# Band attention with a feed-forward network on one Trainium2 core: queries and keys as fp16 halves, and a reordered first batch

## The reference

```python
xn = layernorm(x)
Q, K, V = xn @ Wq + bq, xn @ Wk + bk, xn @ Wv + bv      # 16 heads of 64 columns
scores = einsum('bhid,bhjd->bhij', Q, K)
columns = where(|i - j| <= 64, scores, 0.0)             # outside the band the score is 0, not -inf
out = softmax(columns) @ V                              # so every row still sums over all 1024 columns
attn = out @ Wo + bo
s = xn @ Win + bin_                                     # 512 -> 64
h = relu(s[..., None] * W1 + b1)                        # 16 hidden units for each of the 64
ffn = (einsum('btmh,mh->btm', h, W2) + b2) @ Wout + bout
result = x + attn + ffn
```

## Time and profile before

| | |
|---|---|
| median of three runs | 1953.55 us |
| the profiled execution's own time | 1958.2 us |
| its span, first to last instruction | 1956.5 us |
| busy: PE, PEld, DVE, ACT, POOL | 96%, 52%, 80%, 77%, 82% |
| mean granted TensorE clock | 0.983 |
| score matmuls (L1228), 128 x 12 pairs of heads, mean of one | 283 to 314 ns |
| weight loads of the projections (L1242), fp16, 128 columns | 98 ns |
| L440 POOL, low weights | 715.0 us in 1008 |
| L425 POOL, normalised weights | 629.8 us in 1016 |
| waits of PE for L1021 DVE (K's low half) before scores | 17.9 us, 13 times |
| waits of PE for L979 DVE (an addition) before scores | 16.7 us, 8 times |

### The profile page before, as it was taken

One profiled execution on the slowest core, in us unless ns is written; L12 is line 12 of the kernel. 1 busy time (PEld: TensorE's weight loads), 2 busy tenths in 40 slices (PEclk: granted clock), 3 DMA queues, 4 the chain that ended last, 5 costly groups with the idle time before them and its releaser, 6 DMA issues.

```text
span 1956.5 us, 41951 instructions
## 1 busy us (share of the span) xinstructions
PE 1872.6 (96%) x13699; PEld 1025.4 (52%) x13699; DVE 1555.9 (80%) x4207; ACT 1514.1 (77%) x4089; POOL 1596.0 (82%) x2248
## 2 busy tenths in 40 slices
PE   8889999999999999999999999999999999999995
PEld 4445555455555555555555555555555455555553
DVE  5889886887778877888778877788777897778776
ACT  5988886887777877887777887877777887778774
POOL 3777877987888878988879887898968987888974
PEclk8989999999999999999999999999999999999998
DMA  5676566867588666877658776687757866576666
GB/s 154 145 158 162 118 134 133 193 126 136 114 178 163 130 123 118 187 153 139 125 108 201 156 129 131 121 198 141 136 108 153 193 126 134 115 161 142 138 121 135
DMA packets 745593, 280.56 MB, mean 143 GB/s; under 512 B 682504, under 2 KB 694816, under 8 KB 745376
## 3 DMA queue, kind: packets, MB, share of 16 engines
q1 hardware_dynamic: 745328, 277.87, 68.4%
q10 hardware_dynamic: 48, 0.01, 0.0%
HBM read 84.84 MB, written 25.17 MB: 56 GB/s over the span
## 4 chain that ended last, share of the span: by engine, by line
PE 43%; POOL 32%; ACT 9%; issue 7%; DVE 6%; DMA 2%; SPq 1%; POOLq 0%; DVEq 0%; ACTq 0%
PE ps L1242 22%; POOL probs L425 17%; POOL p_lo L440 11%; PE ps L1257 7%; PE ps L1292 5%; PE ps L1228 4%; ACT probs L576 4%; POOL oT_lo L432 2%; POOL acc L447 2%; PE ps L1279 1%; DMA pT_lo<-p_lo 1%; PE ps L1267 1%; DVE probs L932 1%; ACT p_hi L639 1%; ACT oT_hi L647 1%
## 5 line engine op out<-in xcount | busy, mean ns | idle before, releaser
L1242 PE MATMUL ps<-xT_hi,w_split 128*128 128x512 f16 x3072 | 976.5, 382 | 10.2 <-DMA w_split<-w_kept 5.0
L440 POOL TENSOR_TENSOR p_lo<-probs,p_hi 128x256 f16<-128x256 f32 x1008 | 715.0, 709 | 78.2 <-ACT p_hi L639 0.8
L425 POOL TENSOR_SCALAR probs<-probs,inv_l,neg_e 128x256 f32<-128x256 f32 x1016 | 629.8, 638 | 118.2 <-DVE neg_e L951 117.9
L576 ACT ACTIVATE probs<-probs,neg_max 128x256 f32<-128x256 f32 x1024 | 506.0, 498 | 149.9 <-DVE neg_max L939 149.8
L1242 PE MATMUL ps<-xT_lo,w_split 128*128 128x512 f16 x1536 | 586.5, 382 | 0.0
L1242 PEld LDWEIGHTS ps<-xT_hi,w_split 128*128 128x128 f16 x3072 | 301.9, 98 | 385.1 <-issue 18.2
L932 DVE CUSTOM_DVE_ANT_0 probs<-ps,mask,unit_s 128x256 f32<-128x256 f32 x1024 | 433.2, 477 | 52.5 <-PE ps L1228 32.1
L979 DVE SCALAR_TENSOR_TENSOR acc<-ps,unit_o,acc 128x512 f32<-128x512 f32 x512 | 356.6, 739 | 26.2 <-PE ps L1257 26.2
L639 ACT ACTIVATE p_hi<-probs 128x1024 f16<-128x1024 f32 x256 | 267.8, 1053 | 78.2 <-POOL probs L425 77.7
L1257 PE MATMUL ps<-wo_split,oT_hi 128*128 128x512 f16 x1024 | 306.2, 381 | 8.5 <-POOL oT_lo L432 3.7
L432 POOL TENSOR_TENSOR oT_lo<-o_sum,oT_hi 128x512 f16<-128x512 f32 x128 | 152.7, 1193 | 131.9 <-ACT o_sum L651 131.5
(11 more groups left out here) (117 smaller groups left out, 2514.6 us busy)
## 6 DMA issues: line engine op xcount, KB each, us to landing
w_split<-w_kept SPq DMA_DIRECT2D x168, 256.0 KB, 3.1
acc<-in_L_attn_x SPq DMA_DIRECT2D x14, 1024.0 KB, 6.9
out_x<-acc SPq DMA_DIRECT2D x14, 1024.0 KB, 5.7
wo_split<-wo_kept SPq DMA_DIRECT2D x56, 256.0 KB, 2.9
w_kept<-w_split SPq DMA_DIRECT2D x24, 256.0 KB, 2.7
pT_hi<-p_hi SPq DMA_TRANSPOSE x256, 3.2
pT_lo<-p_lo SPq DMA_TRANSPOSE x256, 3.3
acc<-in_L_attn_x SPq DMA_DIRECT2D x4, 512.0 KB, 5.7
```

The lines of the kernel that those rows point to most:

```text
L425: pool.tensor_scalar(probs[:, h, t], probs[:, h, t], inv_l[:, c:c + 1], neg_e[:, c:c + 1], ALU.mult, ALU.add).then_inc(normed, 1)
L440: pool.tensor_tensor(p_split[lo][:, h, t], probs[:, h, t], p_split[hi][:, h, t], ALU.subtract).then_inc(p_lo, 1)
L576: act.activation(probs[:, h, t], probs[:, h, t], ACT.Exp, bias=neg_max[:, c:c + 1], accum_out=row_sum[:, c:c + 1])
L1242: last = pe.matmul(dst[:], w[wp][:, i, c], xT[xp][:, c, half * LINE:half * LINE + LINE], start=(c == 0 and a == 0), stop=(c == KC - 1 and ...
```

## The change

Queries and keys, both halves, become fp16 instead of the 32-bit type, and the scales of the activations become smaller (`X_SCALE` 2 instead of 2048, `V_SCALE` 2^-7 instead of 2^-17), with a factor `QK_WEIGHT` in the sums of squares of the Q and K weights and biases, so that scaled Q and K fit the type. The scratch tile `squares` becomes fp32. In the steps that prepare the next weights (`split_next`, steps 0 to 6), ScalarE writes Q's next high weights before `weights_high(1, 0)`, and K's second high half and K's next high weights before `weights_high(1, 1)` (in step 0 also before `gather(1)`). On VectorE the scaled biases and units of the next pair become a function of their own, `step_units`, called after `add_output(3)` instead of right after the scales; in the first batch `hidden_unit(2)` goes behind additions 4 and 5; `split_low(n + 1, K_)` goes right behind `qk_low(3)`. The last output scale (step 8) is worked by VectorE at the start of step 9 behind `mask_scores(0)` instead of at the end of step 8, and GpSimd computes its root before the last four low weights instead of behind them.

```diff
@@ -25,7 +25,8 @@
     EPS = 1e-5
-    X_SCALE, W_TOP, V_SCALE, P_SCALE = 2.0 ** 11, 2.0 ** 15, 2.0 ** -17, 2.0 ** 15
+    X_SCALE, W_TOP, V_SCALE, P_SCALE = 2.0, 2.0 ** 15, 2.0 ** -7, 2.0 ** 15
+    QK_WEIGHT = 2.0 ** 6
     BIAS_TOP, W_FLOOR = 2.0 ** 5, 2.0 ** -36
@@ -57,8 +58,8 @@
         wo_kept = nc.dram_tensor("wo_kept", [PAIRS, P, 2, E], F16, kind="Internal").ap()
-        qT = [sb(f"qT_{part}", [P, N], F32R) for part in ("hi", "lo")]
-        kT = [sb(f"kT_{part}", [P, N + 2 * HALF], F32R) for part in ("hi", "lo")]
+        qT = [sb(f"qT_{part}", [P, N], F16) for part in ("hi", "lo")]
+        kT = [sb(f"kT_{part}", [P, N + 2 * HALF], F16) for part in ("hi", "lo")]
         vT = sb("vT", [P, N])
@@ -80,7 +81,7 @@
         ones = sb("ones", [P, P])
-        squares = sb("squares", [P, E], F16)
+        squares = sb("squares", [P, E])
         win_raw = p_split[1][:, 0, 0:2].rearrange("p t w -> p (t w)").bitcast(F32).rearrange("p (k m) -> p k m", m=M)
@@ -475,9 +476,10 @@
                     weights_low(1, 0)
-                    weights_low(1, 1)
                 if n == PAIRS:
                     inverse_root(tops_of_step(n), top_ready, scaled_in(n), root_ready)
+                if attend:
+                    weights_low(1, 1)
                 if k == 1 and proj and b > 0:
@@ -499,7 +501,7 @@
                 act.activation(squares[:], w_raw[:, n % 2, i].rearrange("p k c -> p (k c)"), ACT.Square,
-                               accum_out=top[:, i:i + 1]).then_inc(w_top[i], 1)
+                               scale=1.0 if i == V_ else QK_WEIGHT, accum_out=top[:, i:i + 1]).then_inc(w_top[i], 1)
                 tops.append(i)
@@ -749,11 +751,15 @@
                     qk_high(2)
-                if attend:
-                    weights_high(1, 0)
                 if split_next:
                     split_high(n + 1, Q_)
+                if attend:
+                    weights_high(1, 0)
                 hidden_high(3)
+                if split_next:
+                    qk_high(3)
+                if split_next:
+                    split_high(n + 1, K_)
                 if attend:
@@ -761,10 +767,8 @@
                     gather(1)
-                if proj:
+                if proj and not split_next:
                     qk_high(3)
-                if split_next:
-                    split_high(n + 1, K_)
                 if ln_next and k == 5:
@@ -784,8 +788,8 @@
 
-                dve.memset(f32(kT[part][:, 0:HALF]), 0.0).then_inc(dve_set, 1)
-                dve.memset(f32(kT[part][:, HALF + N:]), 0.0).then_inc(dve_set, 1)
+                dve.memset(kT[part][:, 0:HALF], 0.0).then_inc(dve_set, 1)
+                dve.memset(kT[part][:, HALF + N:], 0.0).then_inc(dve_set, 1)
 
@@ -838,6 +842,8 @@
                 power_of_two(cols, w_scale[:, n + 1, cols], top_split, w_scaled, scaled_in(n))
+
+            def step_units(n):
                 if n < PAIRS - 1:
@@ -865,7 +871,7 @@
                                      bias_qkv[:, V_, :, 0], ALU.mult, ALU.mult).then_inc(bias_squares, 1)
-            dve.scalar_tensor_tensor(bias_squared[:, Q_:], bias_qkv[:, Q_:, :, 0], (X_SCALE * BIAS_TOP) ** -2,
+            dve.scalar_tensor_tensor(bias_squared[:, Q_:], bias_qkv[:, Q_:, :, 0], (QK_WEIGHT / (X_SCALE * BIAS_TOP)) ** 2,
                                      bias_qkv[:, Q_:, :, 0], ALU.mult, ALU.mult).then_inc(bias_squares, 1)
@@ -1019,7 +1025,7 @@
                     dve.scalar_tensor_tensor(part[lo], ps[QK_BANK[s]][:], bias_scaled[:, Q_ + s % 2, k:k + 1],
-                                             f32(part[hi]), ALU.add, ALU.subtract).then_inc(qk_lo, 1)
+                                             part[hi], ALU.add, ALU.subtract).then_inc(qk_lo, 1)
 
@@ -1065,6 +1071,9 @@
                     mask_scores(0)
+                if n == PAIRS + 1:
+                    step_scales(PAIRS)
+                    step_units(PAIRS)
                 if o > 0:
@@ -1113,6 +1122,8 @@
                     add_output(3)
+                if n < PAIRS:
+                    step_units(n)
                 if ln_next and k == 7:
@@ -1129,10 +1140,13 @@
                     split_low(n + 1, Q_)
-                hidden_unit(2)
+                if b > 0:
+                    hidden_unit(2)
                 if out_proj:
...
                     add_output(5)
+                if b == 0:
+                    hidden_unit(2)
                 if ffn and k == 6:
@@ -1142,16 +1156,14 @@
                     qk_low(3)
+                if split_next:
+                    split_low(n + 1, K_)
                 if n == PAIRS:
...
                 row_statistics(3)
-                if split_next:
-                    split_low(n + 1, K_)
                 hidden_unit(3)
...
                     shift_rows(slice(0, T), b + 3)
-                if n == PAIRS:
-                    step_scales(n)
                 if n == 0:
```

More of the change, by code:

```diff
@@ L751, in step @@
                     qk_high(2)
+                if split_next:
+                    split_high(n + 1, Q_)
                 if attend:
                     weights_high(1, 0)
+                hidden_high(3)
                 if split_next:
-                    split_high(n + 1, Q_)
-                hidden_high(3)
+                    qk_high(3)
+                if split_next:
+                    split_high(n + 1, K_)
                 if attend:
```

## The result

The changed kernel takes 1938.36 us (median of 4 runs, 1932.68 to 1939.25); the kernel before took 1952.89 us beside it (4 runs). The ratio is 0.9918, with an interval of 0.9903 to 0.9934: 12.9 to 18.9 us less. Forecast was 1933, with a range of 1915 to 1944. The profiled execution took 1939.03 us, with a span of 1937.3 us, against 1958.2 and 1956.5.

A forecast was written before the change was run, and what follows sets the result against it. Later batches were taken as bound partly by GpSimd, ScalarE and VectorE, partly by TensorE; the start and second batch had excess. Savings 7.7 + 6.5 + 6.6 = 20.8 us took the median 1953.55 to 1933, range 1915 to 1944.

The forecast's parts named there:

- Score matmuls: Groups of 12 fp16 score pairs on TensorE: each 0.22 us shorter, bounds nothing to 0.25 us.
- The entry: First score pair of a group on TensorE: 0.23 us becomes 0.13, saving 0.10 us.
- Five groups a batch on the chain, 7.7 us: Later batches: only five score groups on the chain count, 1.1 us a batch, 7.7 us over seven.
- the whole saving counts: Rival: GpSimd's stretch shrinks with TensorE, later batches give 25 us instead of 7.7; 1915.5 us, chance 0.12.
- The end of step 8, 6.5 us: Root before GpSimd's last four low weights: additions 4.8 us earlier, TensorE's 4.30 us stall and half clock go; 6.5 us saved.
- Step 0 to 1, a loss of 1.9: First batch: gather behind K's second half on ScalarE delays VectorE's K low half; 1.9 us lost.
- Step 1 to 2, +4.1: First batch: K's half 2.4 us earlier, stall 5.79 to 3.4 us, 1.7 us from the clock; 4.1 us gained.
- Steps 3 to 5: First batch: 2.3 us gained at step 2 to 3, 0 at 3 to 4 and 4 to 5.
- nothing is removed from VectorE, only reordered: First batch, 121 to 172 us: VectorE nearly without idle time, so TensorE's shorter wait reappears later; 0 us, bounds 0 to 2.2.
- Steps 5 to 7, +2.1: First batch: 1.6 us from VectorE's shorter wait for K's high weights at step 5 to 6, net 0.5 in steps 6 and 7.
- the cover of GpSimd's queue: Steps 6 and 7: high weights come 0.4 us before GpSimd needs them; without that its queue slips by up to 1 us.
- the first batch as a whole: Sum of the first batch's gains and losses from the new order: 6.6 us saved, bounds -3 to 16.

## Why the prediction was right or wrong

*Score matmuls: right.* 0.22 us a group was forecast, 0.20 measured (1.62 to 1.42). The entry was where most of it lay, as worked out from the weighted sums, and the evictions cost and gave nothing.

*Five groups a batch on the chain, 7.7 us: right in number.* Alone it gave 5.9 us, and 1.1 us a batch in the middle. They aren't quite the five groups that I had named: step 1 of a batch gained for both of its groups, where one was counted, and step 6 shows nothing for the one counted there (its length varies by more than 0.2 us from batch to batch). What I had only argued from the chain, that steps 2 to 5 hide the saving behind GpSimd, is shown: with GpSimd's low weights at 0.41 us, and VectorE's waits for them shorter, the same edit gives 15 to 18 us. The rival "the whole saving counts" (1915.5) fell for the reason given.

*The end of step 8, 6.5 us: right in its mechanism.* The root ended at 299.15, ahead of the last four low weights, and the additions began 4.5 us into step 9 instead of 8.7, 4.2 us sooner where 4.8 were forecast. VectorE waited 0.19 us for the root, and the half clock is gone. VectorE in the changed kernel:

```profile
299.19 0.62 DVE L835 SCALAR_TENSOR_TENSOR top_dif<-top_inv 128x1 f32<-128x1 f32 x1 [0.19 <-POOL top_inv L399]
...
300.67 1.39 DVE L985 SCALAR_TENSOR_TENSOR acc<-ps,unit_o,acc 128x512 f32<-128x512 f32 x2
```

The trace has 6.4 us for step 9, timed runs 2.7 and 6.6.

*Step 0 to 1, a loss of 1.9: right, and too small.* Step 1 grew by 2.8 us, with 3.00 us of stall where about 2.5 was named; moving the gather back takes it away.

*Step 1 to 2, +4.1: right at its place.* The stall for K's half fell from 5.79 to 3.44 us (3.4 forecast) and the half clock from 6.8 to 3.4 us. The step gained 2.6 only, for a wait of 1.6 us for low weights opened further on. The half clock is a matter of the execution: the run without the edit of step 8 has 3.45 us of stall, 6.8 us of half clock and a gain of 1.4.

*Steps 3 to 5: wrong.* The step that failed is "nothing is removed from VectorE, only reordered", with 0 us for steps 3 to 4 and 4 to 5. Steps 3, 4 and 5 became 3.2, 2.6 and 2.0 us shorter, 7.8 in all, where 2.3 were forecast, and the order alone gives 6.6 of that. In step 4 VectorE's busy time fell from 31.6 to 28.2 us with the same operations: unit_part 1.64 to 0.50, the column multiply of xn 4.42 to 2.96, neg_max 1.79 to 0.94. So part of a duration as in the earlier trace rows (1.16 us for the multiply) was no property of the operation but of what GpSimd did beside it. That isn't the whole cause: in step 3 VectorE's busy time fell by 1.5 us only, and in step 5 it stayed at 27.6. The stalls at the heads of steps 3, 4 and 5 shrank from 3.33, 3.24 and 3.34 to 2.28, 1.43 and 0.77 us and the half clocks behind them went (6.8, 3.4 and 3.4 us), which I had not counted either. Putting the units back returned 3.8 of the 7.8 us. How much is VectorE's load and how much the earlier additions stays open.

*Steps 5 to 7, +2.1: wrong.* Step 6 lost 2.6 us in this trace, and 1.0 in the run without the edit of step 8, which has the same stall (3.27 us) but no half clock behind it; its step 2 takes 1.2 us more, and steps 1 to 7 come to the same (216.9 and 217.0 us). I had set the cover of GpSimd's queue at 0.4 us and named the slip, but counted it at nothing. In step 5 GpSimd had stood 3.0 us ahead of the output's low half before the change; after it that gap is gone, since TensorE and ScalarE are sooner and GpSimd isn't, and in step 6 the transposed low weights come last. The faster first batch has run into GpSimd.

That the first batch as a whole came near its forecast (4.6 us of 6.6) is luck, of errors that cancel: against the forecast, steps 3 to 5 gave 5.5 us more, steps 6 and 7 4.8 less, step 2 1.5 less and step 1 0.9 less (in the other run 5.1 more, 3.3 less, 2.7 less and 0.8 less).

## What to carry to other kernels

Take a saving to the chain step by step, and ask in each step which engine is full: here the same edit was worth 6 us while steps 2 to 6 of eight hid it behind GpSimd, and 15 to 18 once GpSimd's low weights were cheap. A duration in a trace belongs to its neighbours as well: before an engine is called full, look whether its cheapest operations come in two sizes. The largest gain that computes everything was a full engine's work moved into its own gap of 4.3 us.

## What the runs showed of the hardware

VectorE's small operations on SBUF operands have a length of their own, and a longer one where they wait for GpSimd. In the kernel before neg_max (128x4) takes 0.170 us in the 97 cases where GpSimd is idle. In 84 cases that began under a running low-weight subtraction it averages 0.314, up to 0.68. Of these 47 were lengthened: every one that began with more than 0.16 us of GpSimd's operation left, but for one that began within 0.002 us of it, and all 47 end 0.02 to 0.03 us after it. The others began in its last 0.12 us, where a wait wouldn't show. Beside the longer bias additions it takes up to 1.26. The additions that read PSUM take 0.73 to 0.75 us whatever GpSimd does (512 cases), and the reciprocals of 128x8 0.20. An example, GpSimd and VectorE in the kernel before:

```profile
148.91 1.16 POOL L432 TENSOR_TENSOR oT_lo<-o_sum,oT_hi 128x512 f16<-128x512 f32 x1 [2.77 <-ACT o_sum L651]
```

```profile
149.04 1.05 DVE L939 TENSOR_SCALAR neg_max<-row_max 128x4 f32<-128x4 f32 x1
```

GpSimd's ends at 150.07, VectorE's at 150.09. The Trainium skill (SBUF — State Buffer, Who interferes with whom) has this as a port pair that VectorE and GpSimd share as an exclusive lock: a VectorE operation with two SBUF inputs (beside a GpSimd operation that reads SBUF), or in one of its two-port modes, waits for the whole running operation of GpSimd, and one with a single SBUF input outside these modes doesn't. The trace agrees, neg_max as a tensor_scalar in a two-port mode being an assumption. My own theory was narrower, that only GpSimd's two-operand operations block, and the run with one-operand low weights refuted it: 8 of 20 neg_max that began under them still waited (the other 12 began in their last 0.10 us), though they took 0.40 us at most, since the operation they waited for was shorter. Under the normalise operations of the kernel before 59 of 63 neg_max began in the last 0.10 us; the other four began 0.03 to 0.04 us into the operation, with 0.53 us of it left, and took 0.18 to 0.19. Why these four didn't wait is open; row_l did in all 11 cases that began with 0.29 us or more left, and in none of the 7 that began with less than 0.12.

GpSimd's 128x256 operation with two tensor operands takes 0.67 us, the one with one tensor operand and constants 0.41, and the normalise (32-bit output, scalars from columns) 0.56. I had expected 0.62 for the second, near the mean of the normalise, 0.64, which holds longer cases, up to 2.69.

The granted clock behind a stall isn't the same in every execution of the same code. The changed kernel and the run without the edit of step 8 do the same up to step 8. Behind stalls of 3.44 and 3.45 us in step 2 the clock was at half for 3.4 and for 6.8 us; behind stalls of 3.28 and 3.27 us in step 6 for 3.4 us and not at all. The steps differ by 1.2 and 1.6 us, so a single step of a single trace isn't known better than that. The run without the edit, the 8.7 us from the end of that stall:

```profile
204.31:213.00 8.69, 8.69 (x92) 5.25 (x94) 8.15 (x35) 8.43 (x32) 6.39 (x10) 1.00 0.77 196
```
